# Seven block products for the query projection of the second layer, from group 3 on

## The chip, the cores and the metric

The kernel runs as one program on one core of a Trainium2 chip. The metric is the device time of one execution in microseconds (us), the median of the executions; lower is better. The trace is of one profiled execution.

## The reference, cut to what matters

The model has two layers over x (16 sequences of 64 tokens, 512 channels; 1024 tokens in all). Each layer adds a gated cross-attention (32 query heads, 8 key heads, 128 channels a head) and then a gated feed-forward. The second layer's attention normalises queries and keys:

```
q = (hidden_states @ Wq.T).reshape(bsz, q_len, H, HD).transpose(0, 2, 1, 3)   # 512 -> 32 x 128
q = _rmsnorm(q, q_norm_w)            # xf * rsqrt(mean(xf*xf) + eps) * w
k = _rmsnorm(jnp.repeat(k, GROUPS, axis=1), k_norm_w)
scores = jnp.einsum('bhqd,bhkd->bhqk', q, k) * scale + attention_mask
probs = softmax(scores)
out = jnp.einsum('bhqk,bhkd->bhqd', probs, v)
return out.transpose(0, 2, 1, 3).reshape(bsz, q_len, H * HD) @ Wo.T
```

`x = x + tanh(g) * ...` of that result closes the attention; the layer norm of x stands ahead of it.

## The kernel before, in words

**Precision.** Large products are made of three matmuls: every operand is split into a high part (rounded to fp32r by a copy on ScalarE) and a low part (original minus high part, on GpSimd or VectorE), and high x high, high x low and low x high are accumulated in one PSUM bank (`three`, lines 226 to 228). So a tile of weights `wq_raw` (128 x 4 x 512) becomes `wq_hi` (L737) and `wq_lo` (L743), `wo_raw` becomes `wo_hi` (L1142) and `wo_lo` (L1310), and the transposed normalised tokens are held as `hT_hi` and `hT_lo` for the whole layer.

**Steps.** The attention runs over 8 groups g (one key head and its four query heads, J = 4) and two token halves h of 512 tokens (8 sequences). A step (g, h) is written per engine in `step` of `att_pe`, `att_act`, `att_pool` and `att_dve`; `att_steps` calls them, (0,0) to (1,1) as separate code, groups 2 to 6 as a loop, group 7 as separate code. Unit u = 2g + h counts the steps. Step u overlaps three units: it projects the queries of u, does scores and softmax of u - 1, and values and output projection of u - 2.

**TensorE in a step of the second layer, in its program order:** scores of u - 1 (`score`, 16 matmuls, bank `ps_s`), then the sums of the squared queries of u - 1 (`folded_sums`, 16 matmuls), then values of u - 2 (`values`, 24 matmuls into `ps_b`), then the queries of u (`project`, four heads of 12 matmuls with 512 columns, banks `ps_q` in turn), then the output projection of u - 2 (`project_out`, four token tiles t of 12 matmuls).

**The others in a step.** VectorE: sums turned (two transposes, eight small copies to `r_s`), scores turned (L1435), scaled by the queries' norms (L1479), masked (L791), maxima (L1490, L1485), low parts of the values' result (`out_low`, L1518, four), folds of the squares (L1470: the two partition halves are added, `fold_squares`), softmax sums (L1502, L1485, L1506), output added to x (`add_output`, L1529, four), probabilities turned (L1512), their low part `p_lo` (L808). GpSimd: `wo_lo` in h = 0 and `wq_lo` in h = 1, the shift of the scores by their maxima (L797), the normalisation (L803). ScalarE: `wo_hi` in h = 0, `wq_hi` of the next group in h = 1, logarithm and exponential of the square sums (L1160, L1162), squares and copy of the queries (L1150, L1153), `o_hi` (L1191), exponentials (L1177), `p_hi` (L1184). SP: loads of wq, wo, keys and values, each behind the semaphores of the buffer's last readers; the load of the wq of group g + 2 waits for `wq_hi` and `wq_lo` of group g + 1.

Each engine works its list in order; semaphores, which count up, are the only links between them. Buffers are laid over one another in SBUF by hand (`alloc` within a closed ExitStack gives an address that the next one uses again).

## Time and profile before

| | us |
|---|---|
| median of 3 executions | 1179.63 (1179.61 to 1179.67) |
| the profiled execution's own time | 1179.01 |
| its span, first to last instruction | 1177.1 |
| TensorE busy | 1169.5 |
| VectorE busy | 880.9 |
| GpSimd busy | 532.9 |
| ScalarE busy | 424.0 |

The second layer's attention steps lie between 735 and 1135 us. Records of matmuls overlap, because the next one starts while the last drains; what a matmul takes of TensorE is the distance between two starts. L12 is line 12 of the kernel; PE is TensorE, PEld its weight loads, DVE VectorE, ACT ScalarE, POOL GpSimd, SP the engine that issues transfers.

### The profile page before, as it was taken

To read this page: it belongs to the slowest core of one execution; us is meant where nothing else is said; L and a number is where in the kernel's file an instruction comes from. 1 tells how busy PE (TensorE), PEld (TensorE's weight loads), DVE (VectorE), ACT (ScalarE), POOL (GpSimd) and SP (SyncE) were. 2 spreads that over 40 slices of the span, in tenths; PEclk is the share of its full clock that TensorE was granted. 3 is DMA by queue.
4 is the path that set the end of the run, shared out by engine and by line. 5 is a ranking of instruction groups with operands and counts; after the bars stand their busy time and mean duration, and the time that the engine had idled before them with its cause. 6 is when DMAs were issued, how large, how long until landed. Compare 5 with 4: busy or idle time off the path is not lost.

```text
span 1177.1 us, 17132 instructions
## 1 busy us (share of the span) xinstructions
PE 1169.5 (99%) x6272; PEld 946.7 (80%) x6272; DVE 880.9 (75%) x1538; ACT 424.0 (36%) x748; POOL 532.9 (45%) x371
## 2 busy tenths in 40 slices
PE   9999999999999999999999999999999999999998
PEld 8888888888788888777788888777777777777776
DVE  4656646898888888889984335798888887888695
ACT  5145152322322222231552123535453443435542
POOL 5522533766667676677463112305242433425410
PEclk9999999999999999999999999999999999999999
DMA  7944735812211221211210003121221221121101
GB/s 286 285 137 159 211 111 162 287 55 81 81 66 59 89 80 45 80 45 45 99 64 36 1 1 107 55 94 57 91 80 45 80 80 54 71 89 39 43 1 72
DMA packets 57315, 106.54 MB, mean 91 GB/s; under 512 B 3633, under 2 KB 36529, under 8 KB 51889
## 3 DMA queue, kind: packets, MB, share of 16 engines
q1 hardware_dynamic: 56736, 104.82, 26.0%
q0 software_dynamic: 384, 1.05, 0.2%
q8 instruction: 32, 0.52, 0.2%
q14 instruction: 19, 0.15, 0.0%
q10 hardware_dynamic: 144, 0.00, 0.0%
HBM read 78.59 MB, written 27.26 MB: 90 GB/s over the span
## 4 chain that ended last, share of the span: by engine, by line
PE 96%; DVE 2%; issue 0%; ACT 0%; DVEq 0%; POOL 0%; POOLq 0%
PE ps_q L226 14%; PE ps_b L226 14%; PE ps_b L228 14%; PE ps_b L227 14%; PE ps_q L227 13%; PE ps_q L228 13%; PE ps_s L978 5%; PE ps_b L1005 4%; PE ps_s L278 1%; PE ps_q L953 1%; PE ps_q L2152 1%; PE ps_b L479 1%; PE ps_s L1847 1%; PE ps_q L529 0%; PE ps_b L529 0%
## 5 line engine op out<-in xcount | busy, mean ns | idle before, releaser
L226 PE MATMUL ps_q<-hT_hi,wq_hi 128*128 128x512 f32 x512 | 203.2, 397 | 0.0
L227 PE MATMUL ps_q<-hT_lo,wq_hi 128*128 128x512 f32 x512 | 199.6, 390 | 0.0
L228 PE MATMUL ps_q<-hT_hi,wq_lo 128*128 128x512 f32 x512 | 199.2, 389 | 0.0
L226 PE MATMUL ps_b<-wo_hi,o_hi 128*128 128x512 f32 x440 | 171.6, 390 | 0.0
L227 PE MATMUL ps_b<-wo_lo,o_hi 128*128 128x512 f32 x440 | 171.2, 389 | 0.0
L228 PE MATMUL ps_b<-wo_hi,o_lo 128*128 128x512 f32 x440 | 171.2, 389 | 0.0
L743 POOL TENSOR_TENSOR wq_lo<-wq_raw,wq_hi 128x512 fp32r<-128x512 f32 x64 | 90.2, 1413 | 112.8 <-ACT wq_hi L737 112.8
L1317 POOL TENSOR_TENSOR qT<-q_t 128x512 f32<-128x512 f32 x64 | 89.8, 1405 | 66.3 <-DVE q_t L1430 60.8
L226 PEld LDWEIGHTS ps_q<-hT_hi,wq_hi 128*128 128x128 f32 x512 | 96.1, 188 | 24.3 <-issue 1.5
L228 PEld LDWEIGHTS ps_q<-hT_hi,wq_lo 128*128 128x128 f32 x512 | 96.1, 188 | 20.3
L227 PEld LDWEIGHTS ps_q<-hT_lo,wq_hi 128*128 128x128 f32 x512 | 96.2, 188 | 18.7
L1310 POOL TENSOR_TENSOR wo_lo<-wo_raw,wo_hi 128x512 fp32r<-128x512 f32 x56 | 83.5, 1507 | 56.4 <-ACT wo_hi L1142 38.3
L1184 ACT ACTIVATE p_hi<-pT 128x1024 fp32r<-128x1024 f32 x32 | 34.0, 1061 | 189.7 <-DVE pT L1512 189.7
L226 PEld LDWEIGHTS ps_b<-wo_hi,o_hi 128*128 128x128 f32 x440 | 82.6, 188 | 18.4 <-issue 1.4
L228 PEld LDWEIGHTS ps_b<-wo_hi,o_lo 128*128 128x128 f32 x440 | 82.6, 188 | 17.1
L227 PEld LDWEIGHTS ps_b<-wo_lo,o_hi 128*128 128x128 f32 x440 | 82.6, 188 | 17.1
L1529 DVE SCALAR_TENSOR_TENSOR x_sb<-ps_b,gates,x_sb 128x512 f32<-128x512 f32 x115 | 81.4, 722 | 18.0 <-PE ps_b L228 17.5
L803 POOL TENSOR_TENSOR p_sb<-p_sb,p_rec 128x1024 f32<-128x1024 f32 x29 | 55.7, 1920 | 83.8 <-DVE p_rec L1506 83.8
L1518 DVE TENSOR_TENSOR o_lo<-ps_b,o_hi 128x512 fp32r<-128x512 f32 x128 | 81.8, 682 | 12.6 <-ACT o_hi L1191 10.7
L1191 ACT ACTIVATE o_hi<-ps_b 128x512 fp32r<-128x512 f32 x128 | 66.5, 607 | 34.0 <-PE ps_b L1005 26.7
L1177 ACT ACTIVATE p_sb<-s_sb,zero_b 128x1024 f32<-128x1024 f32 x32 | 37.2, 1162 | 96.9 <-POOL s_sb L797 93.5
L797 POOL TENSOR_TENSOR s_sb<-s_sb,mx_c 128x1024 f32<-128x1024 f32 x28 | 53.8, 1921 | 32.1 <-DVE mx_c L1485 32.1
(301 smaller groups left out, 2498.0 us busy)
## 6 DMA issues: line engine op xcount, KB each, us to landing
wq_raw<-in_wq SPq DMA_DIRECT2D x16, 1024.0 KB, 4.8
wo_raw<-in_wo SPq DMA_DIRECT2D x16, 1024.0 KB, 4.8
kT<-kT_spill SPq DMA_DIRECT2D x32, 256.0 KB, 4.3
v_hi<-v_hi_spill SPq DMA_DIRECT2D x16, 512.0 KB, 3.7
v_lo<-v_lo_spill SPq DMA_DIRECT2D x16, 512.0 KB, 4.7
v_hi_spill<-vs_hi SPq DMA_DIRECT2D x12, 512.0 KB, 5.4
v_lo_spill<-vs_lo SPq DMA_DIRECT2D x12, 512.0 KB, 6.7
kw_raw<-in_wk SPq DMA_DIRECT2D x4, 1024.0 KB, 9.2
```

The lines of the kernel that those rows point to most:

```text
L226: nc.tensor.matmul(dst, l_hi, r_hi, start=first, stop=False)
L227: nc.tensor.matmul(dst, l_hi, r_lo, start=False, stop=False)
L228: return nc.tensor.matmul(dst, l_lo, r_hi, start=False, stop=last)
L743: nc.gpsimd.tensor_tensor(wq_lo[:, :, j * D:(j + 1) * D], wq_raw[:, :, j * D:(j + 1) * D], wq_hi[:, :, j * D:(j + 1) * D].bitcast(F32), AL ...
L797: eng.tensor_tensor(sc, sc, wide(mx_c[:, :], QB), ALU.subtract).then_inc(c["s_shifted"], 1)
L803: eng.tensor_tensor(pr, pr, wide(p_rec[:, :], QB), ALU.mult).then_inc(c["p_normed"], 1)
L978: last = nc.tensor.matmul(ps_s[par * S:(par + 1) * S, t * JS:(t + 1) * JS], kT[:, h, b:b + S], qT[:, h, :, b:b + S], start=True, stop=True)
L1191: nc.scalar.activation(o_hi[:, 2 * half:2 * half + 2, :, par * S:(par + 1) * S], ps_b[n].rearrange("p (t j q) -> p t j q", t=2, j=J), ACT. ...
L1310: nc.gpsimd.tensor_tensor(lo, wo_raw[:, j, :], hi.bitcast(F32), ALU.subtract).then_inc(c["wo_lo"], 1)
L1317: nc.gpsimd.tensor_tensor(qT[:, h, j, :], q_t1[:, j % 2, :], q_t2[:, j % 2, :], ALU.add).then_inc(c["q_rot"], 1)
L1518: nc.vector.tensor_tensor(o_lo[part], ps_b[n].rearrange("p (t j q) -> p t j q", t=2, j=J), o_hi[part].bitcast(F32), ALU.subtract).then_inc ...
L1529: nc.vector.scalar_tensor_tensor(x_sb[:, i, :], out_bank(u, t)[:, :], gates[:, lay:lay + 1], x_sb[:, i, :], ALU.mult, ALU.add).then_inc(c[ ...
```

## The change

In the second layer, groups 3 to 6 (`woven`; W0 = 3) compute their queries by seven block products. The weights of a group (512 channels x 4 heads) and the tokens of a half are each cut into 2 x 2 blocks (256 channels x 2 heads, 256 channels x 256 tokens). With weight blocks a11, a12, a22, the sums s1 to s4 and mixed token blocks t1 to t4 the seven products are a11 x tokens(0,0), s2 x t2, s3 x t3, a12 x tokens(1,0), s1 x t1, a22 x t4 and s4 x tokens(1,1). Each has 12 matmuls with 256 columns. Four banks hold them, `ps_q` and the two halves of `ps_s`; results are put together by joins on VectorE (PSUM plus SBUF), copies on ScalarE and one sum on GpSimd. The weight sums are built per group on GpSimd, split like the others; the token blocks t1 to t4 once, in steps (1,0) to (2,1), for all groups. Group 7 and groups 0 to 2 keep `project`.

Around it: `folded_sums` goes ahead of the scores in every step with folded squares (units 3 to 13), `project_out` waits for the next unit's folded squares ahead of its last matmul, VectorE's eight copies go and ScalarE takes the logarithm from the turned sums by quadrant, `values` waits for x by halves, the norm weights' product is applied when the keys are staged instead of on each query head, some semaphores are left out, and group 2 and group 6 of this layer become separate code (the loop runs over 3 to 5). In woven units the turned probabilities go to `s_sb` instead of `pT`, whose place holds s2 and s3.

```diff
 (constants) W0 = 3, QT = 256, WD = 2 * D
+        WOVEN_PARTS = ("a11", "s2", "s3", "a12", "s1", "a22", "s4")
+        def woven_high(act, gt, name):        # waits (last use, sum made), then
+            nc.scalar.activation(hi, f, ACT.Copy).then_inc(c["woven_hi"], 1)
+        def woven_low(pool, gt, name):        # waits woven_hi, then
+            nc.gpsimd.tensor_tensor(lo, f, hi.bitcast(F32), ALU.subtract).then_inc(c["woven_lo"], 1)
+        def woven_first_sum(pool, gt):        # waits wq_in
+            nc.gpsimd.tensor_tensor(s1_f, s1_f, woven_parts("a22")[0], ALU.add)
+        def woven_next_sums(pool, gt):
+            nc.gpsimd.tensor_tensor(s2_f[:, :, :], woven_parts("s1")[0], woven_parts("a11")[0], ALU.subtract)
+            nc.gpsimd.tensor_tensor(s3_f[:, :, :], woven_parts("a22")[0], s2_f[:, :, :], ALU.subtract)
+        def woven_last_sum(pool, gt):         # waits q_done 8 * gt if gt != W0
+            nc.gpsimd.tensor_tensor(s4_f[:, :, :], woven_parts("a12")[0], s2_f[:, :, :], ALU.subtract)

         def att_wq_split(sp, lay, n):
+            if lay and n > W0:
+                sp.wait_ge(*att[lay]("woven_hi", 7 * (n - W0)))
+                sp.wait_ge(*att[lay]("woven_lo", 7 * (n - W0)))
+                return
...
+            def project_woven(g, h):          # TensorE
+                def product(bank, name, right, first, last_one=False):
+                    if h == 0:
+                        pe.wait_ge(*c("woven_hi", turn))
+                        pe.wait_ge(*c("woven_lo", turn))
+                    for q in range(2):
+                        for k in range(2):
+                            col = slice(q * D, (q + 1) * D)
+                            dst, closes = bank[:, q * QT:(q + 1) * QT], last_one and (q, k) == (1, 1)
+                            (three matmuls: l_hi x r_hi, l_hi x r_lo, l_lo x r_hi; moving operand r[:, k, :], 256 columns)
+                pe.wait_ge(*c("ssq_t", u))
+                if h == 0:
+                    pe.wait_ge(*c("t_hi", 4))
+                    pe.wait_ge(*c("t_lo", 4))
+                product(ps_q[0], "a11", tokens(0, 0), True).then_inc(c["product"], 1)
+                product(ps_q[1], "s2", mixed(t2_hi, t2_lo), True, True).then_inc(c["product"], 1)
+                pe.wait_ge(*c("s_turned", u))
+                product(ps_h[0], "s3", mixed(t3_hi, t3_lo), True).then_inc(c["product"], 1)
+                pe.wait_ge(*c("copied", 2 * n + 1))
+                product(ps_q[0], "a12", tokens(1, 0), False, True).then_inc(c["q_done"], 1)
+                product(ps_h[1], "s1", mixed(t1_hi, t1_lo), True).then_inc(c["q_done"], 1)
+                pe.wait_ge(*c("joined", 4 * n + 2))
+                product(ps_h[0], "a22", mixed(t4_hi, t4_lo), False, True).then_inc(c["q_done"], 1)
+                pe.wait_ge(*c("copied", 2 * n + 2))
+                product(ps_h[1], "s4", tokens(1, 1), False, True).then_inc(c["q_done"], 1)
...
             def score(u, h, g):
-                pe.wait_ge(*c("q_rot", 4 * u + 4))
                 if lay and folded(u):
-                    pe.wait_ge(*c("q_fold", 4 * u + 4))
+                    folded_sums(u, h)
+                else:
+                    pe.wait_ge(*c("q_rot", 4 * u + 4))
...
+                if woven(lay, g):
+                    project_woven(g, h)
+                    for t in range(PAIRS):
+                        project_out(up, h, g - 1, t, us + 1 if t == PAIRS - 1 else None)   # q_rot, q_fold ahead of the last matmul
+                    return
...
+            def logarithms_by_quadrant():     # ScalarE: 8 ACTIVATE Ln of 32 x 16, r_t -> r_q
...
+            def woven_step(g, h, next_wq):    # ScalarE, in this order (wo_hi x 4 ahead of it in h = 0; parts in [] in h = 1)
+                norms(us); copy of ps_q[0] (copied); out_high 0, 1; [woven_high a11]; out_high 2, 3; [s2]
+                after a12: square and copy of ps_q[0]; after s1: copy of ps_h[1] (copied); [s3]; exponentials(us)
+                square (joined 3); [a12]; square (joined 4); square (c22_made); [s1, a22, s4]; probs_high(us)
...
+            def woven_step(g, h, next_wq):    # GpSimd
+                if h == 0:
+                    for name in WOVEN_PARTS[4:]:
+                        woven_low(pool, g, name)
+                    for j in range(J):
+                        wo_low(g - 1, j)
+                elif building:
+                    woven_low(pool, g + 1, "a11")
+                att_shift(pool, lay, u - 1)
+                (waits copied 2, joined 2)
+                nc.gpsimd.tensor_tensor(qT[:, h, 2:4, late], qT[:, h, 2:4, late], q_sq[:, 2:4, late], ALU.add).then_inc(c["c22_made"], 1)
+                if h and building:
+                    woven_last_sum(pool, g + 1)
+                elif next_wq:
+                    att_wq_low(pool, lay, g + 1, 0)
+                att_normalise(pool, lay, u - 1)
+                if h == 0 and not (isinstance(g, int) and g == G - 2):
+                    woven_first_sum(pool, g + 1)
+                    pool.wait_ge(*c("p_lo", u))
+                    woven_next_sums(pool, g + 1)
+                elif building:
+                    woven_low(pool, g + 1, "s2")
+                    pool.wait_ge(*c("p_lo", u))
+                    woven_low(pool, g + 1, "s3")
+                    woven_low(pool, g + 1, "a12")
...
+                # GpSimd in the steps before (mixed_*: 128 x 1024; first and next are two sums, joined one, low a split)
+                (1,0): att_normalise; wait p_lo; mixed_first(t1)
+                (1,1): att_wq_low 0, 1; att_shift; mixed_joined(t1); att_normalise; att_wq_low 2; wait p_lo; att_wq_low 3; mixed_first(t3)
+                (2,0): wo_low x 4; att_shift; mixed_joined(t3); att_normalise; woven_first_sum; wait p_lo; mixed_next(t2); woven_next_sums
+                (2,1): mixed_low(t1); woven_low a11; att_shift; woven_last_sum; mixed_next(t4); att_normalise; woven_low s2;
+                       wait p_lo; mixed_low(t3), mixed_low(t2), mixed_low(t4); woven_low s3, a12
...
+            def woven_step(g, h):             # VectorE
+                turn_sums(us, 1 - h)
+                turn_scores(us, 1 - h)
+                scale_scores(us)
+                (waits copied 1, product 2) joined(part_b, ps_q[1], part_b)
+                att_mask(dve, lay, us, 1 - h)
+                (waits product 3)           joined(part_d, ps_h[0], part_b)
+                maxima(us)
+                out_low(up, 0)
+                out_low(up, 1)
+                (waits q_done 4u + 3)       joined(qT[:, h, 2:4, early], ps_h[0], part_b)
+                out_low(up, 2)
+                (waits q_done 4u + 4)       joined(part_b, ps_h[1], part_b)
+                sums(us)
+                out_low(up, 3)
+                add_output(up, h, 0)
+                turn_probs(us)
+                fold_woven(u, 0)
+                fold_woven(u, 1)
+                att_probs_low(dve, lay, us)
+                for t in range(1, PAIRS):
+                    add_output(up, h, t)
```

## Rows read from the trace of the kernel before

**Rows 1.** The page: busy us (share) of each engine; the chain's shares.

```profile
PE 1169.5 (99%) x6272; PEld 946.7 (80%) x6272; DVE 880.9 (75%) x1538; ACT 424.0 (36%) x748; POOL 532.9 (45%) x371
...
PE 96%; DVE 2%; issue 0%; ACT 0%; DVEq 0%; POOL 0%; POOLq 0%
```

**Rows 2.** Windows: length; busy us of PE, PEld, DVE, ACT, POOL; clock, DMA share, GB/s.

```profile
840.00:866.10 26.10, 26.10 (x155) 20.68 (x154) 21.00 (x38) 11.26 (x20) 8.94 (x6) 1.00 0.24 85
866.10:892.20 26.10, 26.10 (x155) 20.70 (x154) 21.90 (x38) 11.48 (x20) 10.97 (x6) 1.00 0.15 57
```

**Rows 3.** Timeline of TensorE: start, duration, line, out<-in, tile, count.

```profile
866.09 1.95 PE L978 MATMUL ps_s<-qT,kT 128*64 128x256 f32 x16
867.97 0.66 PE L953 MATMUL ps_q<-q_sq,ones 64*32 64x256 f32 x16
870.18 0.50 PE L226 MATMUL ps_q<-hT_hi,wq_hi 128*128 128x512 f32 x1
...
1001.12 0.39 PE L228 MATMUL ps_q<-hT_hi,wq_lo 128*128 128x512 f32 x1
...
1011.56 0.39 PE L226 MATMUL ps_b<-wo_hi,o_hi 128*128 128x512 f32 x1
```

**Rows 4.** Timeline of TensorE and its weight loads: narrow moving operands.

```profile
869.02 0.28 PE L1005 MATMUL ps_b<-p_hi,v_hi 64*128 64x256 f32 x2
...
869.97 0.28 PE L1005 MATMUL ps_b<-p_hi,v_lo 64*128 64x256 f32 x2
...
1152.46 1.90 PE L2152 MATMUL ps_q<-a_raw,xT 128*128 128x68 f32 x16
1154.16 0.48 PE L226 MATMUL ps_b<-wo_last_a,o_hi 128*128 128x512 f32 x1
...
L227 PEld LDWEIGHTS ps_b<-wo_lo,o_hi x440: 187/188/189, 231.6 to 1127.1; 128*128 128x128 f32 x147
```

**Rows 5.** Timeline of step (5,0): the start of its scores, then VectorE.

```profile
970.38 1.95 PE L978 MATMUL ps_s<-qT,kT 128*64 128x256 f32 x16
...
973.93 1.43 DVE L1457 COPY r_s<-r_t 32x16 f32<-32x16 f32 x8
...
976.75 1.23 DVE L1479 TENSOR_TENSOR s_sb<-s_sb,r_q 128x1024 f32<-128x1024 f32 x1
982.30 1.29 DVE L1518 TENSOR_TENSOR o_lo<-ps_b,o_hi 128x512 fp32r<-128x512 f32 x2
993.06 1.41 DVE L1470 TENSOR_TENSOR q_sq<-q_sq 64x512 f32<-64x512 f32 x2
994.50 1.23 DVE L808 TENSOR_TENSOR p_lo<-pT,p_hi 128x1024 fp32r<-128x1024 f32 x1
```

**Rows 6.** Tile r_s on ScalarE: ns min/median/max, first and last start.

```profile
L1160 ACT ACTIVATE r_q<-r_s,eps_rms x16: 321/322/323, 749.7 to 1123.1; 128x32 f32<-128x32 f32 x16
L1171 ACT ACTIVATE r_s<-r_t x8: 226/228/230, 1121.2 to 1122.9; 32x16 f32<-32x16 f32 x8
```

**Rows 7.** Timeline of VectorE and GpSimd in (2,0), from 818.9.

```profile
820.30 1.23 DVE L1479 TENSOR_TENSOR s_sb<-s_sb,r_q 128x1024 f32<-128x1024 f32 x1
821.56 2.20 DVE L791 TENSOR_TENSOR s_sb<-s_sb,mask_sb 128x1024 f32<-128x1024 f32 x1
823.80 1.22 DVE L1490 TENSOR_REDUCE mx_a<-s_sb 128x32 f32<-128x1024 f32 x1
...
819.08 5.84 POOL L1310 TENSOR_TENSOR wo_lo<-wo_raw,wo_hi 128x512 fp32r<-128x512 f32 x3 [3.04 <-DVE r_s L1457]
```

**Rows 8.** GpSimd by tile and line (ns min/median/max); transfers (KB, us to landing).

```profile
L808 POOL TENSOR_TENSOR p_lo<-pT,p_hi x13: 2382/2397/3464, 243.2 to 550.6; 128x1024 fp32r<-128x1024 f32 x13
...
L797 POOL TENSOR_TENSOR s_sb<-s_sb,mx_c x28: 1917/1921/1922, 202.7 to 1111.3; 128x1024 f32<-128x1024 f32 x28
...
L1310 POOL TENSOR_TENSOR wo_lo<-wo_raw,wo_hi x56: 1270/1291/2361, 225.0 to 1082.1; 128x512 fp32r<-128x512 f32 x56
...
wq_raw<-in_wq SPq DMA_DIRECT2D x16, 1024.0 KB, 4.8
```

More of the change, by code:

```diff
@@ L19 @@
 JS = J * S
+QT = HALF // 2
+WD = 2 * D
+W0 = 3
 SC = PAIRS * JS
@@ new lines, in build, with woven_parts @@
+        WOVEN_PARTS = ("a11", "s2", "s3", "a12", "s1", "a22", "s4")
+        def woven_parts(name):
+            rows, cols = {"a11": (0, 0), "a12": (1, 0), "s1": (0, 1), "a22": (1, 1)}.get(name, (0, 0))
+            own = (slice(None), slice(2 * rows, 2 * rows + 2), slice(cols * WD, (cols + 1) * WD))
+            if name == "s2":
+                return s2_f[:, :, :], s2_hi[:, :, :], s2_lo[:, :, :]
+            if name == "s3":
+                return s3_f[:, :, :], s3_hi[:, :, :], s3_lo[:, :, :]
+            if name == "s4":
+                return s4_f[:, :, :], s4_hi[:, :, :], s4_lo[:, :, :]
+            return wq_raw[own], wq_hi[own], wq_lo[own]
@@ new lines, in woven_high @@
+        def woven_high(act, gt, name):
+            c = att[1]
+            first = isinstance(gt, int) and gt == W0
+            last_use = 2 * gt - 1 - 2 * W0
+            act.wait_ge(*c("wq_in", 16 * (gt + 1)))
+            if name in ("a11", "a12") and first:
+                act.wait_ge(*c("q_done", 8 * gt - 2))
+            elif name in ("s1", "a22") and first:
+                act.wait_ge(*c("q_done", 8 * gt))
+            elif name in ("a11", "s2", "s3") and not first:
+                act.wait_ge(*c("product", 3 * last_use + ("a11", "s2", "s3").index(name) + 1))
+            elif name != "s4" and not first:
+                act.wait_ge(*c("q_done", 8 * gt - 3 + ("a12", "s1", "a22").index(name)))
+            if name[0] == "s":
+                act.wait_ge(*c("s_f", 4 * (gt - W0) + int(name[1])))
+            f, hi, lo = woven_parts(name)
+            nc.scalar.activation(hi, f, ACT.Copy).then_inc(c["woven_hi"], 1)
@@ L1018, in project_out @@
                     hi, lo = wo_parts(lay, g, j)
-                    last = three(out_bank(u, t)[:, :], o_hi[:, t, j, :], o_lo[:, t, j, :], hi, lo, j == 0, j == J - 1)
+                    bank = out_bank(u, t)[:, :]
+                    nc.tensor.matmul(bank, o_hi[:, t, j, :], hi, start=j == 0, stop=False)
+                    nc.tensor.matmul(bank, o_hi[:, t, j, :], lo, start=False, stop=False)
+                    if ahead is not None and j == J - 1:
+                        squares_ready(ahead)
+                    last = nc.tensor.matmul(bank, o_lo[:, t, j, :], hi, start=False, stop=j == J - 1)
                 last.then_inc(c["y_done"], 1)
@@ new lines, in step @@
+                if lay and isinstance(g, int) and (g, h) == (2, 0):
+                    for j in range(J):
+                        wo_low(1, j)
+                    att_shift(pool, lay, us)
+                    mixed_joined(t3_f, t3_t, 6)
+                    att_normalise(pool, lay, us)
+                    woven_first_sum(pool, W0)
+                    pool.wait_ge(*c("p_lo", us + 1))
+                    mixed_next(t2_f, (1, 1), t1_f, 8, 3)
+                    woven_next_sums(pool, W0)
+                    return
@@ L1434, in turn_scores @@
                 dve.wait_ge(*c("scored", u + 1))
+                if lay and not (isinstance(u, int) and (u < 4 or u == 2 * G - 1)):
+                    dve.wait_ge(*c("p_lo", u))
                 nc.vector.transpose(s_sb[:, :], ps_s[:, :]).then_inc(c["s_turned"], 1)
@@ L1534, in step @@
                 if before_closing(lay, g, h):
+                    return
+                if woven(lay, g):
+                    woven_step(g, h)
                     return
```

330 lines of the change are left out of this document (282 added, 48 removed).

## The prediction

> **What bounds the kernel now.** Read the page's busy times first: TensorE is busy in 1169.5 us, 99% of the span, and the chain of waits is TensorE for 96% [rows 1]. Since matmul records overlap, busy alone proves little. So I cut the second layer into its steps by the start of each step's scores, and asked for the busy time of every engine in each [rows 2]. A step (group g, token half h) lasts 26.1 us, TensorE has no idle time in it, and its granted clock is 1.00, the 2.4 GHz level. TensorE's own timeline of one step shows why [rows 3]: scores, square sums and values take 4.1 us (866.09 to 870.18), the 48 query matmuls start 0.227 us apart (1001.12 to 1011.56 is 46 of them: 10.44 us), and 48 output matmuls follow at the same spacing. 4.1 + 10.9 + 10.9, and small gaps where the tile shape changes, make 26.07. Only fewer TensorE microseconds can shorten such a step; only another engine's lateness can lengthen it. VectorE is busy for 21 to 22 of the 26 us, GpSimd for 9 to 11 [rows 2].
>
> **What the narrow matmuls cost.** A woven step has 7 products of 12 matmuls with 256 columns, 84 for 48 of 512. The trace has no 128x128 matmul of 256 columns. The nearest rows are the value matmuls: two of 64 rows side by side, each with its own 128-column weights, go every 0.119 us (eight in 0.95 [rows 4]). And 16 matmuls of full 128x128 weights with only 68 columns start within 1.70 us, 0.106 each, so a full weight load comes in no more than that [rows 4]. I take 0.118, between it and half of 0.227: 84 x 0.118 = 9.9 for 10.9, 0.97 us less a step. The bounds: 0.113 for exactly half (1.4 less a step); if 0.188, the record of one weight load, were not hidden behind its neighbour, 84 x 0.188 = 15.8, 4.9 more a step. Eight steps are woven, (3,0) to (6,1). If nothing else moves: 8 x 0.97 = 7.8 us.
>
> **The order of the square sums.** They go ahead of the scores; VectorE's eight small copies (1.43 us) go, and ScalarE takes logarithms by quadrant instead. VectorE now scales the scores 6.4 us after the step's start (976.75 against 970.38) [rows 5]. After: sums read at 0.8, transposes to 1.7, eight pieces at 0.228 (the eight quadrant copies of the last step are the same form on ScalarE [rows 6]) and an exponential of 0.32 [rows 6]: 3.9, in h = 0 4.6, as the four wo_hi splits of that step go ahead on ScalarE. TensorE never waits in these steps, so the 2 us are slack and worth nothing alone. The wait moved ahead of the last output matmul queues that matmul behind the folds: it costs nothing while the fold ends 0.4 us before the step does; it ends at 24.1 (994.47) of 26.07 now [rows 5].
>
> **The woven step on the other engines.** VectorE loses 1.43 (copies) and gets four joins of the form of out_low (PSUM and SBUF in, 512 elements), 1.29 a pair [rows 5]: +2.6. The folds become two of twice the length, 1.2 each (p_lo's 1.23 [rows 5] for the same number of columns). Together 23.1 us in a step of 25. GpSimd gets, per group, 7 splits and 4 sums for 4 splits, and one sum a step: +9 x 1.29 = 11.6 us a pair of steps.
>
> These two engines get in each other's way, and the change puts more of it in. Where three wo_lo of 1.29 run beside VectorE's scaling and mask, the three take 5.84 instead of 3.87, and the mask 2.20 instead of 1.23 [rows 7]. Transposes, reductions and reads of PSUM are not stretched; operations with both inputs in SBUF are. I price this as taking turns. The Trainium skill says it as a rule that speaks against the change (SBUF — State Buffer, Who interferes with whom): a VectorE instruction with two SBUF inputs and a GpSimd instruction that reads SBUF exclude each other, and the second one blocks fully. By that rule, the trace agrees: 1.97 us more on GpSimd, 0.97 on VectorE, no sharing of bandwidth.
>
> Walked through in program order with these durations, from a step's start:
> - h = 1: scale 7.2, join 7.9, mask 9.1, join 9.8, maxima 11.8, out_low 13.0 (TensorE wants it at 14.1), shift 13.8, exponential 15.0, last out_low 18.2 (wanted at 19.5), probabilities turned 20.8, folds 23.2 (wanted 24.7). TensorE sets the step: 26.07 - 0.97 = 25.1.
> - h = 0: GpSimd comes with nine splits in a row (s3, a12, s1, a22, s4, four wo_lo; 9 x 1.25 = 11.3) and takes turns with scale, mask and maxima, so that it ends at 13.9, the shift at 15.9, the exponential at 17.1, the reciprocal at 19.5 and the third and fourth out_low at 20.2 instead of 19.55: a stall of 0.65. Step 25.75.
> A pair is 50.85 for 52.14. The margins are tenths: 0.1 us for wo_lo.
>
> **Getting there: groups 1 and 2, and step (3,0).** Four mixed token tiles are built by GpSimd: ten sums and four splits of 128x1024. A split of this size on GpSimd is there in layer one: p_lo, 2.39 us [rows 8]. 14 x 2.39 = 33.5 us in four steps; the shift, with one broadcast input, and the longest p_lo bound one at 1.92 and 3.46 [rows 8].
> Step (1,1) has room. In (2,0), after p_lo of the step before, come one split, 2 big sums, 4 wo_lo, shift, a big sum, normalise: 1.3 + 4.8 + 5.1 + 1.9 + 2.4 + 1.9 = 17.4, and turns with VectorE of some 7: it fits in 26.07 if no wait falls badly. In (2,1) there are 2 big sums, 2 small, a big split, a small one, shift, a small sum, 2 big sums and normalise: 5 x 2.39 + 4 x 1.3 + 2 x 1.92 = 21. The turns with VectorE's scale, mask, folds, p_lo and the small maxima and sums are 1.2 + 1.2 + 2.8 + 1.2 + 1.6 = 8, and the transpose between is 1.25: 30 us from p_lo to p_lo. The folds behind them gate the last matmul. p_lo ends at 25.3 (995.73 [rows 5]) and may end at 27.1 before the fold ahead of it holds that matmul, 1.7 of slack. With (2,0) on time and (2,1) 3.9 too long, the two grow by 2.2; with (2,0) 3.2 late as well (its shift waits for the four wo_lo, its last out_low for the turns), by 5.4. I take 3.9.
> Then (3,0): TensorE waits for all four t_lo ahead of its first product. Three of them stand on GpSimd behind p_lo of (2,1), which ends 1.0 into (3,0): 1.0 + 3 x 2.39 + one turn of 1.2 = 9.4. TensorE would be there at 3.9 (the 4.1 of rows 3 less the first gap): stall 5.5. Behind them are the nine small splits, 11.3 and two turns, 2.0: wo_lo at 22.7. The products end at 9.4 + 9.9 + 0.1 = 19.4: stall 3.3. The shift stands behind the splits and makes the fourth out_low 0.7 late. The step: 25.1 + 9.5 = 34.6. Bounds for it: without any lateness in (2,1) and no turns, p_lo ends at -0.7, t_lo at 6.5 and wo_lo at 17.8 for 16.5: 3.9; with (2,1) at its worst, 12.
>
> **At nothing:** the product of the norm weights moves into the staging of the keys (the same instruction with a scale; cover is gone only if the key blocks wait for ScalarE: under 0.3 us, one instruction's length); the small load of these weights moves ahead of x on SP's queue (0.3 us of issue); semaphores left out; the mask and the queries' bank waits. SP's load of the next wq waits for the last split of the woven parts, now 6 to 7 us into h = 0 (in (3,0) 16), lands 4.8 us later [rows 8] and is wanted behind normalise at 21: hidden; without that cover it would delay the sums, not TensorE, by some us.
>
> **The sum.** The eight steps: 8 x 26.07 = 208.6 before; after 34.6 + 4 x 25.1 + 3 x 25.75 = 212.2. With 3.9 in group 2: +7.5 us. The profiled execution is 1179.01 us (span 1177.1 and 1.9 around it): 1186.5. The median is 0.6 above it: 1186.5 to 1187.1. I say 1187.
>
> **Rivals.**
> - The saving arrives. GpSimd's queue is shorter than I walk it (VectorE's small operations find gaps, the sums run in other idle time), entry costs its lower bound 3.9 and the rest is TensorE's: -7.8 + 3.9 = -3.9, 1175 to 1176; with the entry hidden as well 1171 to 1172. For it: GpSimd is busy for a third of these steps now. Against: the three t_lo cannot start before p_lo, and 7.2 us is more than 3.9. Chance 0.24.
> - The steady steps are bound by VectorE and GpSimd taking turns: 23.1 us of work plus waits for r_q, for normalise and for three or four turns. Each h = 0 step gets 1.5 to 2 us of stall and each h = 1 some 0.5: +4 x 1.3 + 4 x 0.5 on the forecast, 1194. It decides once wo_lo is later than 14.1 in every group. For it: my margins of 0.1 to 0.6. Against: h = 1 catches up by over 1 us. Chance 0.15.
> - Weight loads are not hidden behind 256 columns: at 0.188, 8 x 4.9 more than the old steps, 1225 and above. For it: the record of a load is 0.188. Against: 0.106 for full loads [rows 4]. Chance 0.03. The Trainium skill has a rule to this side (TensorE: Matmul & The Clock Gate, Part 3): weight loads overlap running matmuls only in other row groups. By it the 512-column spacing could not be 0.227 with its load hidden, and the trace disagrees.
> - The narrow matmul costs what it takes to break even, 0.130, with entry hidden: 1179 to 1180, nothing gained. Chance 0.03.
>
> **How the numbers follow.** The forecast has 0.55. Its own range is 1179 to 1192: -7.8 and three stalls of 0.65 with an entry of 3.9 + 2.2 to 12 + 5.4. The range is 1173 to 1196, which leaves out the far ends of the first and third rival. A measurement of this kernel tells 0.2%, 2.4 us, from no change. Faster by more: the first rival and a little of the forecast, 0.25; within: 0.06; slower: 0.69.
>
> **What would show it.** TensorE idle or spaced out ahead of the first product of (3,0), released by GpSimd's t_lo, about 5 us; again ahead of its first output matmul, released by wo_lo. Steps (3,1), (4,1) of 25.1; (4,0), (5,0), (6,0) of 25.7. Spacing 0.118 in the products. GpSimd's two-input operations stretched to 2.3. I am wrong if t_lo is done by 4 us into (3,0), or if the steady steps differ from 25.1 and 25.75 by over half a us.

## The result, and the profile after

| | before | after |
|---|---|---|
| median of the runs side by side, us | 1179.62 (4 runs) | 1192.12 (4 runs, 1190.23 to 1192.68) |
| the profiled execution | 1179.01 | 1192.26 |
| its span | 1177.1 | 1190.4 |

The changed kernel is slower: ratio 1.0105, 95% interval 1.0087 to 1.0122. The page after, beside [rows 1]: busy times, and the chain's shares by engine.

```profile
PE 1167.9 (98%) x6560; PEld 956.8 (80%) x6560; DVE 898.0 (75%) x1458; ACT 454.8 (38%) x840; POOL 615.3 (52%) x421
...
PE 80%; DVE 10%; issue 5%; POOL 3%; ACT 1%; DVEq 0%; POOLq 0%
```

TensorE has 288 matmuls more and is busy 1.6 us less, yet the span is 13.3 us longer: TensorE now stands still. The chain, TensorE for 96% before, is so for 80%, with VectorE (10%), issue (5%) and GpSimd (3%) for most of the rest. The windows of (2,1), (3,0), (3,1) and (4,0) (columns as in [rows 2]):

```profile
843.97:873.44 29.47, 26.61 (x167) 20.61 (x152) 26.25 (x31) 16.97 (x33) 24.80 (x12) 1.00 0.13 45
873.44:908.68 35.24, 28.45 (x203) 24.29 (x188) 27.85 (x35) 12.79 (x26) 28.22 (x18) 0.90 0.20 68
908.68:933.81 25.13, 25.13 (x203) 21.62 (x188) 20.63 (x32) 14.82 (x30) 11.62 (x8) 1.00 0.15 53
933.81:959.75 25.94, 25.42 (x203) 21.67 (x188) 22.21 (x32) 12.68 (x26) 19.00 (x14) 1.00 0.25 91
```

(3,1) is what was hoped for: TensorE busy throughout, and 0.94 us shorter. (2,1) and (3,0) have GpSimd busy for 25 and 28 us, VectorE for 26 and 28, and TensorE idle in between. All steps by their length, in us:

| step | before | forecast | after |
|---|---|---|---|
| (1,0) and (7,0) together (square sums cross the border of both) | 53.52 | 53.5 | 53.87 |
| (1,1) | 26.23 | 26.2 | 27.00 |
| (2,0) and (2,1) | 52.14 | 56.0 | 57.94 |
| (3,0) | 26.07 | 34.6 | 35.24 |
| (3,1), (4,1), (5,1) | 26.07 | 25.1 | 25.13 |
| (4,0), (5,0), (6,0) | 26.07 | 25.75 | 25.94, 25.89, 25.77 |
| (6,1) | 26.07 | 25.1 | 26.67 |

The differences add up to the 13.3 us of the span. What TensorE waited for (line and tile, releaser: us in total, times, longest):

```profile
PE ps_b L1194 <- DVE q_sq L1839: 5.5, 4, 2.5
PE ps_b L1190 <- DVE o_lo L1894: 4.2, 4, 2.8
PE ps_q L1087 <- POOL t_lo L1607: 4.0, 1, 4.0
PE ps_b L1194 <- DVE q_sq L1847: 1.3, 1, 1.3
```

The first line is the last output matmul held by the folds, up to (2,1); the third and the 2.8 of the second are (3,0); the last is (6,1). GpSimd's and VectorE's timelines of (3,0) (columns as in [rows 7]) show the queue:

```profile
873.83 6.99 POOL L1607 TENSOR_TENSOR t_lo<-t_f,t_hi 128x1024 fp32r<-128x1024 f32 x3 [2.82 <-DVE p_lo L921]
880.78 2.27 POOL L825 TENSOR_TENSOR s_lo<-s_f,s_hi 128x512 fp32r<-128x512 f32 x1
883.01 3.77 POOL L825 TENSOR_TENSOR wq_lo<-wq_raw,wq_hi 128x512 fp32r<-128x512 f32 x3
886.73 2.28 POOL L825 TENSOR_TENSOR s_lo<-s_f,s_hi 128x512 fp32r<-128x512 f32 x1
888.97 5.00 POOL L1577 TENSOR_TENSOR wo_lo<-wo_raw,wo_hi 128x512 fp32r<-128x512 f32 x4
894.09 1.91 POOL L910 TENSOR_TENSOR s_sb<-s_sb,mx_c 128x1024 f32<-128x1024 f32 x1
```

```profile
888.38 1.20 DVE L1866 TENSOR_REDUCE mx_a<-s_sb 128x32 f32<-128x1024 f32 x1
889.61 4.40 DVE L1861 TENSOR_TENSOR mx_c<-mx_a 32x32 f32<-32x32 f32 x4
894.04 1.29 DVE L1894 TENSOR_TENSOR o_lo<-ps_b,o_hi 128x512 fp32r<-128x512 f32 x2
```

GpSimd runs without a gap from 873.83 to 896. The three t_lo end at 880.8, and TensorE starts its first product at 881.19. Then the nine splits. Beside the last four of them VectorE's four tiny maxima of 32x32, which take 0.77 us elsewhere, take 4.40 (each of them ends 0.04 us behind one of the four wo_lo), and o_lo behind them comes at 894. TensorE's first output matmul starts at 895.69.

### The profile page after: what moved, and what is told of

Read it like the earlier page. It is cut to its first block, busy times and chain, and to the rows that moved or that the text cites. A ratio compares the mean times of both kernels' runs of the same rounds, so it can differ in the third digit from the quotient of the medians.

```text
span 1190.4 us, 17765 instructions
## 1 busy us (share of the span) xinstructions
PE 1167.9 (98%) x6560; PEld 956.8 (80%) x6560; DVE 898.0 (75%) x1458; ACT 454.8 (38%) x840; POOL 615.3 (52%) x421
## 4 chain that ended last, share of the span: by engine, by line
PE 80%; DVE 10%; issue 5%; POOL 3%; ACT 1%; DVEq 0%; POOLq 0%
PE ps_q L253 9%; PE ps_q L255 9%; PE ps_q L254 9%; PE ps_b L1190 7%; PE ps_b L1194 7%; PE ps_b L1191 7%; PE ps_b L255 4%; PE ps_b L253 4%; PE ps_b L254 4%; PE ps_s L1140 4%; PE ps_b L1170 4%; POOL p_sb L916 1%; PE ps_q L1087 1%; DVE mx_c L1861 1%; DVE mx_a L1866 1%
## 5 line engine op out<-in xcount | busy, mean ns | idle before, releaser
L253 PE MATMUL ps_q<-hT_hi,wq_hi 128*128 128x512 f32 x384 | 152.7, 398 | 0.0
L254 PE MATMUL ps_q<-hT_lo,wq_hi 128*128 128x512 f32 x384 | 149.8, 390 | 0.0
L255 PE MATMUL ps_q<-hT_hi,wq_lo 128*128 128x512 f32 x384 | 149.5, 389 | 0.0
L1577 POOL TENSOR_TENSOR wo_lo<-wo_raw,wo_hi 128x512 fp32r<-128x512 f32 x56 | 81.1, 1470 | 13.4 <-ACT wo_hi L1320 13.4
L253 PEld LDWEIGHTS ps_q<-hT_hi,wq_hi 128*128 128x128 f32 x384 | 72.1, 188 | 18.8 <-issue 1.5
L255 PEld LDWEIGHTS ps_q<-hT_hi,wq_lo 128*128 128x128 f32 x384 | 72.1, 188 | 15.4
L852 POOL TENSOR_TENSOR wq_lo<-wq_raw,wq_hi 128x512 fp32r<-128x512 f32 x48 | 70.4, 1474 | 26.2 <-ACT wq_hi L769 23.4
L254 PEld LDWEIGHTS ps_q<-hT_lo,wq_hi 128*128 128x128 f32 x384 | 72.2, 188 | 13.9
L1378 ACT ACTIVATE p_hi<-pT 128x1024 fp32r<-128x1024 f32 x21 | 22.3, 1061 | 133.3 <-DVE pT L1888 133.3
```

The costliest lines, as they stand in the source:

```text
L253: nc.tensor.matmul(dst, l_hi, r_hi, start=first, stop=False)
L254: nc.tensor.matmul(dst, l_hi, r_lo, start=False, stop=False)
L255: return nc.tensor.matmul(dst, l_lo, r_hi, start=False, stop=last)
L852: nc.gpsimd.tensor_tensor(wq_lo[:, :, j * D:(j + 1) * D], wq_raw[:, :, j * D:(j + 1) * D], wq_hi[:, :, j * D:(j + 1) * D].bitcast(F32), AL ...
L1577: nc.gpsimd.tensor_tensor(lo, wo_raw[:, j, :], hi.bitcast(F32), ALU.subtract).then_inc(c["wo_lo"], 1)
```

## The experiments

**Is the queue of low splits what (3,0) loses?** First only the three late splits are left out.

```
-                    pe.wait_ge(*c("t_lo", 4))
+                    pe.wait_ge(*c("t_lo", 1))
-                    mixed_low(t3_lo, t3_hi, t3_f, 2)     # likewise t2, t4; the products read t_hi
```

> Left out: the low parts of the mixed tokens t2, t3, t4 (three splits of 128x1024 on GpSimd behind p_lo of step (2,1)); their products read the high part in place of the low one. Everything else as in the changed kernel. Theory (TensorE waits in (3,0) for GpSimd's queue, first for t_lo, then for what stands behind it): GpSimd gets 7.2 us back, so (3,0) falls from 35.2 to the length of the other h = 0 steps, 25.9 to 27.5, and the whole by 8 to 9 us, to about 1183.5. Rival (VectorE's lateness out of (2,1) sets (3,0), t_lo only coincides): (3,0) stays above 30 and the whole falls by under 5 us.

Measured 1185.02 us, ratio 1.0043 (1.0026 to 1.0059): 7.1 less than the changed kernel, where I had expected 8 to 9. (3,0) fell from 35.24 to 26.89, while (2,1) in front of it did not get shorter (29.95 for 29.47). So it is GpSimd's queue, and not lateness out of (2,1), that (3,0) loses.

**All of the mixed tokens' work left out (the 14 operations on GpSimd and four copies on ScalarE), and, in a second kernel, the woven products left out.**

```
-                    mixed_first(t1_f, t1_t, (0, 1), (0, 0))     # and the other 13 operations
-                product(ps_q[1], "s2", mixed(t2_hi, t2_lo), True, True)
+                product(ps_q[1], "s2", tokens(0, 1), True, True)
```

> Left out: all mixed token tiles (ten sums and four splits of 128x1024 on GpSimd, four copies on ScalarE); the products read plain token blocks. Theory (the 33.5 us on GpSimd pay for all that is lost in (1,1) to (3,0)): (1,1), (2,0), (2,1) go back to 26.1 to 26.3, (3,0) to about 25.9, and the whole is 1179.6 + 0.35 + 1.5 in (6,1) less 8 x 26.07 - (4 x 25.13 + 4 x 25.9), 4.5: about 1177. Rival (the new order of sums or the waits ahead of the last output matmul cost something in these steps by themselves): the steps before (3,0) stay 0.3 us or more too long each, and the whole stays above 1179.

```
         def woven(lay, g):
-            return lay == 1 and not (isinstance(g, int) and (g < W0 or g == G - 1))
+            return False
```

> The change without the seven products: all groups projected as before, no mixed tokens, no weight sums; kept are the sums of squares ahead of the scores, the logarithms by quadrant on ScalarE, the wait ahead of the last output matmul, the norm weights in the keys. Theory: TensorE sets the steps, nothing is gained or lost in them, and (1,0) is 0.35 longer for the wait's place: 1179.6 to 1180.3. Rival (the new order gives something back through the shorter chain): below 1179. Rival (eight pieces of 0.33 instead of 0.228 us on ScalarE hold something): above 1181.

Without the mixed tokens' work: 1178.19, ratio 0.9989 (0.998 to 0.9999), where I had expected 1177. Every step from (1,1) to (2,1) is back at 26.07 or 26.08; (1,0) is 27.40. (3,0) is 27.05 and not the 25.9 that I had expected, and (3,1), (4,1) and (5,1) are 25.28, 0.15 more than in the changed kernel, which no run explains. So about 14 us of the changed kernel is this one-off work, and the woven steps themselves gain very little. With the new order alone: 1179.79, ratio 1.0002 (0.9992 to 1.0012): the square sums ahead of the scores and the logarithms by quadrant are worth nothing by themselves; (1,0) is 27.40, every step from (1,1) to (6,1) 26.07 or 26.08.

**The wait moved back behind the last output matmul.**

```
+                    if waits_in_scores(u):               # u in (2, 3, 4, 12, 13)
+                        squares_ready(u)
-                    if ahead is not None and j == J - 1:
+                    if ahead is not None and j == J - 1 and not waits_in_scores(ahead):
```

> The changed kernel with one edit: for units 2, 3, 4, 12 and 13 the wait for folded squares stands ahead of the sums again, behind the last output matmul, not ahead of it. In (1,0), (1,1), (2,0), (2,1) (unit 5 keeps its place) and (6,1) that matmul waited. Theory: each of (1,0), (1,1), (2,0), (6,1) gets back what the matmul takes, 0.2 to 0.35 us: the whole falls by about 1. Rival (the place of the wait is worth nothing, TensorE resumes at the same time): under 0.3.

1192.81, ratio 1.0103 (1.0083 to 1.0123): a miss. (1,0), (1,1) and (6,1) fell by 0.4 each, but (2,1) grew by 0.4 and (7,0) by 0.94. Why these two give the time back is not shown.

**The splits of group 7 in (6,1).**

```
                 elif next_wq:
+                    pool.wait_ge(*c("p_lo", u))
                     for j in range(1, J):
```

> One added wait: GpSimd takes the three wq_lo splits of group 7 in (6,1) only after the low probabilities of that half, as it does in the plain steps. Theory (those splits stand beside VectorE's folds, which took 4.51 us for the two instead of 2.47, and held TensorE for 1.3 us): (6,1) falls from 26.67 to about 25.3 us, the whole from 1192.1 to about 1190.7. Rival (the splits are then late for (7,0)'s projections): (6,1) falls but (7,0) grows from 26.48 by as much, and the whole stays at 1192.

1191.18, ratio 1.0097 (1.0081 to 1.0112); (6,1) fell from 26.67 to 25.13, (7,0) stayed at 26.48. The 0.9 us of the median are within the scatter of both kernels' runs; the step is what shows it. The timelines of GpSimd and VectorE there, the changed kernel first:

```profile
1081.53 4.79 POOL L852 TENSOR_TENSOR wq_lo<-wq_raw,wq_hi 128x512 fp32r<-128x512 f32 x3
...
1082.88 4.51 DVE L1847 TENSOR_TENSOR q_sq<-q_sq 64x1024 f32<-64x1024 f32 x2
```

```profile
1087.64 3.79 POOL L852 TENSOR_TENSOR wq_lo<-wq_raw,wq_hi 128x512 fp32r<-128x512 f32 x3 [5.12 <-DVE p_lo L921]
...
1083.84 2.47 DVE L1848 TENSOR_TENSOR q_sq<-q_sq 64x1024 f32<-64x1024 f32 x2
```

Side by side the two take 4.79 and 4.51 us; apart 3.79 and 2.47. TensorE wanted the folds.

**One long operation or two short ones.**

```
+            def in_halves(out, left, right, op):
+                nc.gpsimd.tensor_tensor(out[:, 0:1], left[:, 0:1], right[:, 0:1], op)
+                return nc.gpsimd.tensor_tensor(out[:, 1:2], left[:, 1:2], right[:, 1:2], op)
```

> The sums, differences and low splits of the mixed tokens (14 operations of 128x1024 on GpSimd) are each issued as two of 128x512, same work and order. Theory (VectorE's two-input operations wait until the GpSimd instruction under way has ended, so that the longest single instruction is what a fold or a maximum loses): the waits of VectorE in (1,1), (2,0) and (2,1) fall by about half, each of those steps by 0.3 to 1 us, (3,0) stays near 35 because its queue is as long, and the whole is 1189 to 1191. Rival (what counts is how long GpSimd holds the port in all, and two halves hold it longer than one whole, 2 x 1.29 against 2.39): no step falls, (3,0) grows by about 1 us, and the whole is 1192 to 1194.

1190.31, ratio 1.0095 (1.008 to 1.0111). (1,1) fell to 26.07 and (2,0) to 27.45, 0.9 and 1.0 less; (2,1) was 29.62 for 29.47 and (3,0) 34.53 for 35.24. In (1,1), VectorE's folds in the kernel before, then the folds and GpSimd's sum beside them in the changed kernel, then here:

```profile
801.26 1.98 DVE L1470 TENSOR_TENSOR q_sq<-q_sq 64x512 f32<-64x512 f32 x2
```

```profile
802.78 2.86 POOL L1597 TENSOR_TENSOR t_f<-t_f,t_t 128x1024 f32<-128x1024 f32 x1
...
801.41 4.78 DVE L1839 TENSOR_TENSOR q_sq<-q_sq 64x512 f32<-64x512 f32 x2
```

```profile
801.99 3.67 DVE L1843 TENSOR_TENSOR q_sq<-q_sq 64x512 f32<-64x512 f32 x2
...
803.35 1.76 POOL L1590 TENSOR_TENSOR t_f<-t_f,t_t 128x512 f32<-128x512 f32 x1
```

The two folds took 1.98 us before and take 4.78 and 3.67 now. The first of them takes 0.7 us more in both kernels, behind the shift of the scores. The second waits until the GpSimd sum under way has ended: taken singly it lasts 0.69 us before, 2.78 beside a whole sum and 1.67 beside a half, so 2.1 and 1.0 us more. The length of the single operation counts where the queue has gaps. In (3,0), which has none, the sum of the queue should count; the halves left that step within 0.7 us.

**Each product with its own wait for its split.**

```
-                if h == 0:
-                    pe.wait_ge(*c("t_hi", 4))
-                    pe.wait_ge(*c("t_lo", 4))
+                        sums = {"s2": 3, "s3": 2, "s1": 1, "a22": 4}.get(name)
+                        if sums:
+                            pe.wait_ge(*c("t_hi", sums))
+                            pe.wait_ge(*c("t_lo", sums))
```

> The one wait of TensorE for all four low splits of the mixed tokens, ahead of the first product of (3,0), is taken apart: each product waits for its own split (s2 for the third, s3 for the second, s1 for the first, a22 for the fourth). GpSimd's order is untouched. If the wait for t_lo itself (4.0 us) is what (3,0) loses, (3,0) falls by about 2.5 to 4 us, to 31 to 33, and the whole to about 1189. If (3,0) is held by GpSimd's queue as a whole (four low splits, then wo_lo and the shift, on which VectorE's low splits of the output and TensorE's output product hang), the time comes back as a longer wait for o_lo and (3,0) stays within 1 us of 35.2. I expect the second for more than half: (3,0) 34 to 35.

1191.36, ratio 1.0102 (1.0087 to 1.0118); (3,0) 33.79. The one wait of 4.0 us became two of 0.6 and 1.3, the wait for o_lo stayed 2.8, and the step is 1.45 us shorter. So more than half of the 4.0 us came back, as expected, though the step lies below the 34 to 35 that I had said. In this profile the clock also fell in another place, at the start of (3,0) and not at its products, so the 1.45 us is not the waits' alone.

**What the clock takes.** The granted clock of (3,0) is 0.90. In windows of 2 us of the changed kernel:

```profile
878.00:880.00 2.00, 0.00 (x0) 0.00 (x0) 1.09 (x1) 0.83 (x3) 2.00 (x2) 1.00 0.02 4
880.00:882.00 2.00, 0.81 (x6) 0.84 (x7) 1.91 (x1) 0.00 (x0) 2.00 (x2) 0.96 0.00 0
882.00:884.00 2.00, 2.00 (x12) 2.00 (x11) 0.00 (x0) 0.34 (x1) 2.00 (x2) 0.50 0.03 8
884.00:886.00 2.00, 2.00 (x14) 2.00 (x14) 0.18 (x1) 2.00 (x5) 2.00 (x3) 0.68 0.00 0
...
894.00:896.00 2.00, 0.31 (x1) 0.34 (x2) 1.97 (x5) 0.00 (x0) 1.91 (x2) 0.88 0.50 94
896.00:898.00 2.00, 2.00 (x6) 1.52 (x6) 1.91 (x3) 1.96 (x3) 1.25 (x2) 0.50 0.99 418
898.00:900.00 2.00, 2.00 (x8) 1.61 (x7) 1.89 (x7) 0.75 (x2) 0.29 (x1) 0.77 0.37 143
```

Right behind each of the two standstills the granted clock is 0.50, the 1.2 GHz level, for some 3.4 us; output matmuls then start 0.43 us apart, not 0.227. The next experiment fills both standstills.

```
+                def keep_busy(bank):
+                    if isinstance(g, int) and (g, h) == (W0, 0):
+                        for n_ in range(32):
+                            nc.tensor.matmul(bank[:, 0:QT], hT_hi[:, n_ % 4, tok[0]][:, 0:D], hT_hi[:, 0, tok[1]], start=True, stop=True, skip_group_check=True)
+                keep_busy(ps_q[0])                       # ahead of the wait for t_lo
+                keep_busy(ps_h[1])                       # ahead of product s4
```

> In (3,0) TensorE's two standstills (4.0 us ahead of the first product, 2.8 ahead of the first output matmul) are filled with matmuls whose result nobody reads: 32 of 256 columns ahead of the wait for t_lo, and 32 ahead of the last product s4, 3.8 us each at 0.118. No other engine's work changes. In the changed kernel the granted clock fell to 1.2 GHz for 3.4 us behind each standstill. If the step loses time to that, the clock stays at 1.00 here; the products then end 1.5 us sooner, which buys nothing, since VectorE's o_lo is what the output matmuls wait for and its time is set by GpSimd; behind o_lo the output matmuls go at 0.227 from the start and not at 0.43: (3,0) 33.5 to 33.8 instead of 35.24, the whole about 1190.5. Rival (the lower clock hid behind waits in both places): (3,0) stays at 35.2 or grows by what the extra matmuls delay.

1192.72, ratio 1.0108 (1.0091 to 1.0125), where I had expected 1190.5: for the whole a miss. (3,0) is 34.08 in the profile, for the 33.5 to 33.8 expected. Its windows from the step's start to behind the first output matmuls:

```profile
874.00:876.00 2.00, 2.00 (x22) 0.81 (x19) 2.00 (x4) 1.96 (x4) 1.34 (x1) 0.50 0.00 0
876.00:878.00 2.00, 2.00 (x14) 0.87 (x10) 0.59 (x2) 1.55 (x6) 2.00 (x2) 0.64 0.00 0
...
894.00:896.00 2.00, 2.00 (x19) 2.00 (x18) 1.97 (x3) 0.00 (x0) 1.87 (x2) 1.00 0.16 41
896.00:898.00 2.00, 2.00 (x16) 1.91 (x15) 1.95 (x4) 0.99 (x1) 2.00 (x2) 1.00 0.90 291
```

Behind the filled places the clock is 1.00, and a fall comes at the start of the step, after the 2.5 us wait of (2,1), where I had put nothing. From the first output matmul to its end the step takes 11.55 us and not 12.99: 1.44 us of (3,0) is the clock behind the second standstill. Two other observations agree: without filling, the fall is there in all four kernels whose wait for o_lo in (3,0) was 2.8 us or more, and the kernel with halves, whose wait there was 1.3 us, shows none and takes 11.6 us from its first output matmul on. The products' low clock was hidden: o_lo comes 20.21 us behind GpSimd's first t_lo in the changed kernel (894.04 less 873.83) and 20.35 here (895.01 less 874.66), where the products run at 1.00.

```profile
895.01 1.29 DVE L1903 TENSOR_TENSOR o_lo<-ps_b,o_hi 128x512 fp32r<-128x512 f32 x2
897.35 0.40 PE L1199 MATMUL ps_b<-wo_hi,o_hi 128*128 128x512 f32 x1
```

The filling cost something too. The first output matmul starts 2.34 us behind the first o_lo (897.35 less 895.01), against 1.65 in the changed kernel, because the extra matmuls and product s4 behind them are not through earlier; without these 0.7 us the step would take some 33.4 (an estimate from these numbers). The whole did not get faster beyond what the runs scatter (1190.2 to 1193.3).

What makes the clock fall stays open. The 2.5 us wait of (2,1) stands in the profiles of seven kernels; a fall follows it in four (no late splits, the splits of group 7, own waits, and here) and none in three. In the run on the splits of group 7 the wait for t_lo was 2.4 us, and with nothing filled in the clock stayed at 1.00 behind it (first line). In the six-step run below it stayed at 1.00 behind a wait of 3.4 us (second line). So the length of the standstill alone does not decide, and that filling the first place was needed is not shown.

```profile
882.00:884.00 2.00, 1.94 (x16) 1.98 (x17) 0.77 (x1) 0.16 (x1) 2.00 (x2) 1.00 0.00 0
930.00:932.00 2.00, 1.71 (x14) 1.74 (x15) 0.00 (x0) 0.00 (x0) 2.00 (x3) 1.00 0.00 0
```

**Later, and spread.** Three kernels move the start of the woven products to a later group and spread the 14 operations over more steps, most of them behind the low probabilities, two to a step or three. The second and third also have own waits and halves, as above; the third is shown against the second.

```
-W0 = 3
+W0 = 4                                   # in (1,1), behind the low probabilities:
+                        mixed_joined(t1_f, t1_t, 3)
+                        mixed_first_high(t3_f, (1, 1), (0, 1))
```

> The woven products begin with group 4 and not group 3, so that six steps have them and not eight; group 3 is plain, the mixed tokens' sums are spread over (1,0) to (3,1), two or three to a step and behind the low probabilities, and the three wq_lo splits of group 7 stand behind them too. Theory (the steady steps gain about 0.5 us on average and the entry's 14 us is GpSimd's big operations standing ahead of work that TensorE waits for): (1,1) to (3,1) take 26.1 to 26.5 each, (4,0) about 26, the woven steps 25.1 and 25.9, and the whole is 1176 to 1178, under the kernel before (1179.6). Rival (the big operations hold VectorE wherever they are put): the entry still costs 3 us or more over its six steps, and the whole is 1179 or more.

```
+                        in_halves(...)           # all 14
+                    if isinstance(g, int) and g == W0:
+                        mixed_low(t2_lo, t2_hi, t2_f, 3)
```

> From the run with woven products from group 4 on: own waits as in the run before, the big operations in halves, and never more than two whole big operations in one step behind the low probabilities ((1,0) to (3,0) two each, (3,1) one and one, (4,0) the splits t2 and t4, one of them between wo_lo's). Theory (a step has room for about two, and what is past that is lost in the next step): (3,0) 26.1 instead of 28.6, (3,1) about 26.5 instead of 27.9, (4,0) 28 to 29 instead of 30.8, and the whole 1179 to 1181. Rival (three were not the trouble in (2,1), it is that the next sums and the lows of the first woven group come on top in (3,0) and (3,1)): (3,1) and (4,0) stay as they were and the whole is 1183 or more.

```
-W0 = 4
+W0 = 5
```

> Woven products from group 5 on, so four steps have them; the fourteen big operations in halves, two to a step over (1,0) to (3,1), one in (4,0) and one in (4,1), own waits. Theory: (1,1) to (4,0) 26.07, (4,1) about 26.1, (5,0) 26 to 28, (5,1), (6,0), (6,1) 25.13, 25.8, 25.13: the whole 1177.5 to 1179.5, a little under the kernel before or level with it. Rival (the entry costs some microseconds wherever it lies): 1180 or more.

Measured 1185.69 (ratio 1.0057, 1.0043 to 1.0071), 1186.2 (1.0058, 1.0045 to 1.0072) and 1185.38 (1.0051, 1.0038 to 1.0065): all faster than the changed kernel, and none reaches what I expected (1176 to 1178, 1179 to 1181, 1177.5 to 1179.5). By steps: (1,1), (2,0) and (2,1) are 26.07 or 26.08 in all three, with two operations at the head of each at no cost. (3,0) was 28.55 with three ahead of it, and lost 1.6 us even with two (27.71, 27.75), (4,0) of the last one too (27.60). The first woven step stood at 30.75, 35.32 and 30.44; in the one of 35.32, t2_lo and t4_lo stand among the nine splits of that step, and TensorE waits 3.4 and 3.7 us for t_lo. The kernel with four woven steps shows its own reasons in GpSimd's timeline of (4,0) and (4,1):

```profile
925.32 3.52 POOL L1584 TENSOR_TENSOR wo_lo<-wo_raw,wo_hi 128x512 fp32r<-128x512 f32 x2
932.06 1.92 POOL L910 TENSOR_TENSOR s_sb<-s_sb,mx_c 128x1024 f32<-128x1024 f32 x1 [3.22 <-DVE mx_c L1907]
933.93 3.42 POOL L1584 TENSOR_TENSOR wo_lo<-wo_raw,wo_hi 128x512 fp32r<-128x512 f32 x2
...
960.14 1.30 POOL L825 TENSOR_TENSOR wq_lo<-wq_raw,wq_hi 128x512 fp32r<-128x512 f32 x1 [7.06 <-ACT wq_hi L818]
...
975.27 1.28 POOL L1597 TENSOR_TENSOR t_lo<-t_f,t_hi 128x512 fp32r<-128x512 f32 x1 [2.80 <-DVE p_lo L921]
```

I had written two wo_lo behind the shift, so that they wait for VectorE's maxima although GpSimd is idle for 3.2 us; and t_lo stood behind p_lo at the head of the critical queue, although GpSimd is idle for 7.1 us in the middle of (4,1). Both are places of mine, mended in the last version (shown against the one with four steps), together with the wait for the squares of unit 2, put back as in the experiment on it:

```
-                    wo_low(3, 0)                        # (4,0); (3,0) likewise
-                    wo_low(3, 1)
+                    for j in range(J):
+                        wo_low(3, j)
                     att_shift(pool, lay, us)
-                    wo_low(3, 2)
-                    wo_low(3, 3)
+                    mixed_low(t4_lo, t4_hi, t4_f, 4)      # (4,1), ahead of a11
+                return isinstance(u, int) and u == 2      # the wait in front of the sums again
```

> The run with four woven steps and three of its places mended: in (3,0) and (4,0) all four wo_lo splits stand ahead of the shift, as in the plain steps; the split t4_lo moves from behind the low probabilities of (4,1) to the 7.1 us in which GpSimd waits for wq_hi of a11 there; and TensorE's wait for the squares of unit 2 stands in front of its sums again. Theory (the mixed tokens' work costs nothing where GpSimd has idle time that ends before VectorE's folds and before what TensorE waits for): (1,0) 27.0 instead of 27.4, (3,0) and (4,0) 26.07 instead of 27.75 and 27.60, (5,0) about 27 instead of 30.4, and the whole 1185.4 - 0.4 - 1.7 - 1.5 - 3.4 = 1178.4, 0.1% under the kernel before. Rival (the first woven step costs some microseconds for other reasons, wq_lo and s_lo splits beside VectorE's low splits of the output among them): (5,0) stays over 29 and the whole is 1180.5 or more.

1177.68 (11 runs, before 1179.16 in 15), ratio 0.9989 (0.998 to 0.9998): faster than the changed kernel, and by 0.1% than the one before. With so many runs the interval just leaves out 1, although 0.1% is under the 0.2% that I named for a measurement. The steps bear it out: from (5,0) to (6,1) they are 1.5 us shorter than before. Its windows of (3,0), (3,1), (4,1), (5,0) and (5,1):

```profile
867.33:893.41 26.08, 26.08 (x154) 20.67 (x152) 21.78 (x32) 13.59 (x28) 15.88 (x11) 1.00 0.14 51
893.41:919.48 26.07, 26.07 (x154) 20.67 (x152) 19.99 (x32) 14.69 (x30) 13.99 (x11) 1.00 0.26 91
945.55:971.63 26.08, 26.08 (x154) 20.68 (x152) 22.12 (x30) 15.42 (x32) 15.34 (x11) 1.00 0.15 51
971.63:998.44 26.81, 25.38 (x190) 21.67 (x188) 23.74 (x33) 12.47 (x26) 19.97 (x14) 1.00 0.25 90
998.44:1023.57 25.13, 25.13 (x190) 21.62 (x188) 21.74 (x35) 15.10 (x31) 13.38 (x10) 1.00 0.14 53
```

The work of the same 14 operations now costs nothing in the plain steps. Each of the three edits shows in its own step: (1,0) 27.01 for 27.40, (3,0) and (4,0) 26.07 for 27.75 and 27.60, (5,0) 26.81 for 30.44. The first woven step still has 0.74 us more than a plain one; (5,1), (6,0) and (6,1) gain 0.94, 0.37 and 0.94.

## Why the prediction was right, and what was mis-sized

The direction and the mechanism held: slower by an entry that costs more than eight steps save. The size did not: the forecast was +7.5 us on the profiled execution; it is +13.3. Step by step:

- **Products.** 0.118 us apart (eleven starts from 912.83 to 914.01). Steps (3,1), (4,1), (5,1) 25.13 for 25.1, TensorE without a gap. Right; the rivals of unhidden weight loads and of break-even fall.
- **h = 0 of the steady groups.** 25.94, 25.89 and 25.77 for 25.75, with the wait for o_lo of 0.5. Right, and the rival of steady steps bound by turns falls with it.
- **(3,0).** 35.24 for 34.6. The lateness until the first output matmul, forecast as 5.5 + 3.3 + 0.7 = 9.5, is 10.11 - 1.44 = 8.7: a wait of 4.0 for t_lo, 2.8 for o_lo, and between them products stretched by the lower clock. I had the waits longer, and named wo_lo as the releaser where it is o_lo, held back by the same queue through the maxima. The clock was no term at all: 1.44 us. That 34.6 comes within 0.6 of the step is partly luck, since the lateness had 0.8 too much and the clock was missing.
- **(2,0) and (2,1).** Term 3.9, measured 5.8, just over the upper bound of 5.4. The waits are at the last output matmul, behind the folds, as forecast.
- **"Step (1,1) has room", and the wait moved ahead "costs nothing".** Wrong. (1,1) lost 0.77 us: I had counted no turns for it, and the folds beside the shift and the big joined sum took 4.78 us for 1.98. With the sum in halves the step is 26.07. (1,0) and (7,0) together lost 0.35, of which the wait is the cause: with it back in front of the sums (1,0) is 27.01 instead of 27.40 (the last version against the one before it).
- **(6,1).** 26.67 for 25.1. I counted it with the h = 1 steps, but its three wq_lo of group 7 do not stand behind p_lo as the other late splits do; one line shows it, and one wait takes 1.54 us away. This is more than the half us that I had named as the sign of being wrong about the steady steps; the other six kept within 0.2.
- **Logarithms by quadrant.** Eight take 2.64 us, 0.33 each, where I had 0.228 from the copies [rows 6]. No path went over them: the order alone made no difference.

The terms missed are 1.1 in group 1, 1.9 in group 2, 0.6 in (3,0), 0.3 in the steady h = 0 and 1.6 in (6,1): 5.5 of the 5.8 us. The main rival, that the saving arrives, put a hidden entry at 1171 to 1172. The kernel without the 14 operations has that entry at no cost and takes 1178.19, about 1 us less than before. That rival has 0.97 us from each of eight steps; here (3,1), (4,1) and (5,1) give 0.8 each and the steady h = 0 steps 0.1 to 0.3, while (3,0) costs 1.0, (6,1) 0.6 and (1,0) with (7,0) 0.4. That the 1.0 of (3,0) is its nine other splits is argued, not shown.

The rule of the Trainium skill in SBUF — State Buffer, Who interferes with whom, which the prediction priced, agrees with the traces in the places shown above: (1,1), (3,0) and (6,1). It reaches down to operations of 32x32, 4.40 us for 0.77. Of the clock, the Trainium skill (TensorE: Matmul & The Clock Gate, Part 1) states that the granted clock follows how busy the engine has lately been. The trace agrees in the second place of (3,0): 0.50 behind a standstill of 2.8 us, 1.00 when it is filled. The first place and the wait of (2,1) leave open what decides it, as shown above.
